# x loaded a second time, transposed, and scaled by GpSimd; half of k's maxima subtracted inside ScalarE's exp

## The reference

```python
xn = _ln(x, ln_w, ln_b)
q = xn @ Wq + bq
k = xn @ Wk + bk + (1.0 - src_mask) * -1000000.0
q = softmax(q.reshape(b, t, h, dh), axis=-1)      # 8 heads of 32 channels
k = softmax(k.reshape(b, t, h, dh), axis=1)       # over the 64 positions
v = ((xn @ Wv + bv) * src_mask).reshape(b, t, h, dh)
att = einsum('bnhd,bnhl->bhdl', k, v)
y = einsum('bnhd,bhdl->bnhl', q, att).reshape(b, t, d)
scale, shift = split((silu(emb) @ W_emb + b_emb)[:, None, :], 2, axis=2)
hh = _ln(y, ln2_w, ln2_b) * (1.0 + scale) + shift
out = x + silu(hh) @ W_out + b_out
```

## Time and profile before

| | |
|---|---|
| median of 3 runs | 322.28 us (321.87 to 325.95) |
| profiled execution, its time | 323.25 us |
| profiled execution, its span | 321.4 us |
| busy, TensorE / VectorE / GpSimd / ScalarE | 96% / 86% / 71% / 60% of the span |
| mean granted clock of TensorE | 0.992 of full speed |

### The profile page before, as it was taken

One profiled execution on the slowest core, in us unless ns is written; L12 is line 12 of the kernel. 1 busy time (PEld: TensorE's weight loads), 2 busy tenths in 40 slices (PEclk: granted clock), 3 DMA queues, 4 the chain that ended last, 5 costly groups with the idle time before them and its releaser, 6 DMA issues.

```text
span 321.4 us, 14568 instructions
## 1 busy us (share of the span) xinstructions
PE 308.0 (96%) x5664; PEld 263.4 (82%) x5664; DVE 275.1 (86%) x749; ACT 193.0 (60%) x378; POOL 229.4 (71%) x276
## 2 busy tenths in 40 slices
PE   7899989999999999999999999999999999999974
PEld 6577867887988898988888898988889898988864
DVE  3775989889797998989898989989898989988883
ACT  1449384667486575668485675757575765756360
POOL 2170459778778687878887787878788887889550
PEclk9999999999999999999999999999999999999979
DMA  7930301050412204040403214050403110010023
GB/s 213 353 110 0 100 4 37 2 167 4 130 38 72 92 8 155 2 163 0 131 32 97 66 42 121 0 163 0 145 19 119 44 65 0 12 55 2 4 68 131
DMA packets 21706, 23.84 MB, mean 74 GB/s; under 512 B 1073, under 2 KB 19121, under 8 KB 21682
## 3 DMA queue, kind: packets, MB, share of 16 engines
q1 hardware_dynamic: 20192, 21.89, 22.0%
q10 hardware_dynamic: 1490, 1.62, 1.5%
HBM read 15.12 MB, written 8.39 MB: 73 GB/s over the span
## 4 chain that ended last, share of the span: by engine, by line
PE 82%; DVE 7%; DMA 4%; issue 2%; ACT 1%; POOL 1%; SPq 1%; POOLq 1%; DVEq 0%
PE bv L890 27%; PE bk L890 27%; PE by L890 13%; PE by L966 4%; PE by L945 4%; PE bv L957 4%; PE by L1026 4%; DMA x_all<-in_x 4%; DVE ystat L769 1%; DVE xstat L621 1%; DVE y_s L760 1%; DVE xt_lo L789 1%; DVE k_t L800 1%; ACT xhat L550 1%; POOLq L45 1%
## 5 line engine op out<-in xcount | busy, mean ns | idle before, releaser
L349 POOL TENSOR_TENSOR k_t<-k_t,kmax 128x512 f32<-128x512 f32 x32 | 34.4, 1074 | 26.3 <-DVE kmax L804 26.3
L496 ACT ACTIVATE k_t<-k_t 128x512 f32<-128x512 f32 x32 | 20.0, 626 | 44.5 <-POOL k_t L349 44.5
L267 POOL TENSOR_TENSOR z_s<-z_s,mod_shift 128x512 f32<-128x512 f32 x30 | 30.7, 1043 | 14.2 <-DVE z_s L720 14.2
L360 POOL TENSOR_TENSOR h_lo<-h_s,h_hi 128x512 fp32r<-128x512 f32 x30 | 38.5, 1306 | 2.9 <-ACT h_hi L513 2.3
L368 POOL TENSOR_TENSOR x_all<-x_all,bo_all 128x1024 f32 (+1 forms) x16 | 38.9, 2434 | 0.0
L550 ACT ACTIVATE xhat<-x_all,xr 128x256 f32 (+1 forms) x62 | 32.2, 591 | 4.6 <-DVE xr L632 3.1
L416 POOL TENSOR_SCALAR y_s<-y_s,yr 128x256 f32<-128x256 f32 x60 | 32.7, 558 | 2.5 <-POOL yr L413 2.2
L800 DVE SCALAR_TENSOR_TENSOR k_t<-off,bk 128x512 f32<-128x512 f32 x32 | 21.9, 683 | 14.5 <-PE bk L890 14.5
L890 PE MATMUL bv<-w_o_hi,h_hi 128*128 128x256 f32 x120 | 32.3, 288 | 0.0
L890 PE MATMUL bv<-w_o_lo,h_hi 128*128 128x256 f32 x120 | 32.2, 290 | 0.0
L520 ACT ACTIVATE xt_hi<-by 128x512 fp32r<-128x512 f32 x32 | 17.4, 597 | 23.4 <-PE by L1026 23.4
(11 more groups left out here) (128 smaller groups left out, 867.2 us busy)
## 6 DMA issues: line engine op xcount, KB each, us to landing
x_all<-in_x SPq DMA_DIRECT2D x15, 512.0 KB, 4.6
out<-x_all SPq DMA_DIRECT2D x15, 512.0 KB, 3.2
off<-in_mask_rows SPq DMA_DIRECT2D x16, 256.0 KB, 3.3
x_all<-in_x SPq DMA_DIRECT2D x2, 256.0 KB, 3.7
z_s<-in_w_emb ACTq DMA_DIRECT2D x1, 512.0 KB, 9.7
h_s<-in_w_emb ACTq DMA_DIRECT2D x1, 512.0 KB, 12.3
out<-x_all SPq DMA_DIRECT2D x2, 256.0 KB, 2.6
y_s<-in_wk ACTq DMA_DIRECT2D x1, 256.0 KB, 3.8
```

Of the source, the lines that this page charges most:

```text
L267: return eng.tensor_tensor(z, z, mod_shift[:, c, span(g, GB)].unsqueeze(2).broadcast_to([P, GB, SEQ]), ALU.add)
L349: nc.gpsimd.tensor_tensor(kk, kk, kmax[:, c, :].unsqueeze(2).broadcast_to([P, GB, SEQ]), ALU.subtract).then_inc(ksub_d, 1)
L360: nc.gpsimd.tensor_tensor(h_lo[:, c, :], h_s[:, c, :], h_hi[:, c, :].bitcast(fp32), ALU.subtract).then_inc(hlo_d, 1)
L496: nc.scalar.activation(k_t[:, parity, c, :], k_t[:, parity, c, :], ACT.Exp).then_inc(kexp_d, 1)
```

## The change

x is handed over a second time, transposed in memory (x_t, channels by rows). Each group's block of it is loaded into xt_raw (channels in partitions). Rows now lie along the free dimension, so rstd and bias have to be the same in all partitions: xr[:,2:4], 128 partitions x 2 x 4 numbers, is stored to a small tensor in memory (rows_stored), and loaded again as a broadcast to all partitions (rows_loaded, 128 x 2 x 512). GpSimd multiplies and adds in place (x_scaled, two instructions for each block c), ScalarE copies to xt_hi (x_high), VectorE subtracts to xt_lo. xhat and its transposes on TensorE remain for group 0 alone. The statistics of x and x_rstd are made for group i+3 in turn i, where it was i+1; x is loaded three groups ahead (S says that group i+3 exists).

For block 1 of k, the mask is applied with the sign turned, so that the tile holds -k; VectorE takes the minimum, which is minus the maximum of k. ScalarE subtracts inside the exp: eight activations of 64 columns, one for each batch, with scale -1 and the minimum as bias. k_shifted on GpSimd remains for block 0.

The four instructions that normalise y_s go from GpSimd to ScalarE (y_hat_all, at the head of the next turn), but for the last turn. The orders change: on GpSimd two shifts, k_shifted, h_low 0, x_scaled 0, h_low 1, x_scaled 1, y_scale, x_rstd of i+3, x_biased; on VectorE x_stats stands between the two h_products, x_low after q's tiles 2 and 3; on ScalarE y_hat_all leads and x_high ends the turn. Two more turns at the end are written out.

```diff
+            def rows_stored(g, parity):
+                wait(sp, xr_d, 4 * g + 4)
+                wait(sp, rows_in, 16 * g - 32)
+                sp.dma_start(rows_dram[parity].rearrange("k (t p) -> p k t", p=P), xr[:, 2:4, :], allow_slow_non_contiguous=True
+                             ).then_inc(rows_out, 16)
+            def rows_loaded(g, parity):
+                wait(sp, rows_out, 16 * g)
+                wait(sp, xs_d, 2 * g - 2)
+                sp.dma_start(rows[:, :, :].rearrange("p k n -> p (k n)").unsqueeze(1),
+                             rows_dram[parity:parity + 1].rearrange("o k n -> o (k n)").unsqueeze(0)
+                             .broadcast_to([P, 1, 2 * GT])).then_inc(rows_in, 16)
...
+            def body(i, par, N, F, B, O, S):        # SP
+                if S:
+                    if not (isinstance(i, int) and i < 0):
+                        wait(sp, xstat_d, 4 * i + 5)
+                    load_x(i + 3, 1 - par)
                 if N and not (isinstance(i, int) and i < 1):
-                    wait(sp, xstat_d, 4 * i)
-                    load_x(i + 1, 1 - par)
                     wait(sp, kadd_d, 2 * i)
                     load_off(i + 1, 1 - par)
+                if not (isinstance(i, int) and i + 2 >= G):
+                    rows_stored(i + 2, par)
                 if O and not (isinstance(i, int) and i < 3):
                     store(i - 3)
+                if not (isinstance(i, int) and i + 2 >= G):
...
+                        load_xt(i + 2, par)
+                    rows_loaded(i + 2, par)
...
+            def x_scaled(g, parity, c):             # GpSimd
+                if c == 0:
+                    wait(pool, rows_in, 16 * g)
+                    wait(pool, xt_in[parity], 8 * (g + parity))
+                xc = xt_raw[:, parity, c, :]
+                nc.gpsimd.tensor_tensor(xc, xc, rows[:, 0, :], ALU.mult).then_inc(xm_d, 1)
+                wait(pool, xm_d, 2 * g + c - 1)
+                nc.gpsimd.tensor_tensor(xc, xc, rows[:, 1, :], ALU.add).then_inc(xs_d, 1)
...
+                if O:                               # GpSimd's body
+                    shifts(i - 2)
+                k_shifted(i, par)
+                for c in range(C):
+                    if O:
+                        h_low(i - 2, c)
+                    if N:
+                        x_scaled(i + 1, 1 - par, c)
+                if B:
+                    y_scale(i - 1)
...
+                if S:
+                    x_rstd(i + 3)
+                if not last_turn(i):
                     x_biased(i)
...
+            def k_exp_shifted(g, parity):           # ScalarE
+                wait(act, kmax_d, 2 * g + 2)
+                for n in range(GB):
+                    kk = k_t[:, parity, 1, n * SEQ:n * SEQ + SEQ]
+                    last = nc.scalar.activation(kk, kk, ACT.Exp, scale=-1.0, bias=kmax[:, 1, n:n + 1])
+                last.then_inc(kexp_d, 1)
...
+            def k_masked(i, par, c):                # VectorE
...
+                nc.vector.scalar_tensor_tensor(k_t[:, par, c, :], off[:, par, :], (-1000000.0, 1000000.0)[c], bk_[c][:, :],
+                                               ALU.mult, (ALU.add, ALU.subtract)[c]).then_inc(kadd_d, 1)
...
+            def x_low(i, c, full):                  # VectorE; full is xt_raw[:, 1 - par, c, :], for group 0 bt[c]
+                wait(dve, hi_d, 2 * i + c + 1)
+                nc.vector.tensor_tensor(xt_lo[:, c, :], full, xt_hi[:, c, :].bitcast(fp32),
+                                        ALU.subtract).then_inc(lo_d, 1)
...
+                if B:                               # VectorE's body
+                    kv_scaled(i - 1)
+                if O:
+                    h_product(i - 2, 0)
+                if S:
+                    x_stats(i + 3, 1 - par)
+                if O:
+                    h_product(i - 2, 1)
...
-                if F:                               # TensorE's body
+                if first(i):
+                    pe.wait_ge(xhat_d, 4)
                     for c in range(C):
-                        if c == 0:
-                            wait(pe, xhat_d, 4 * i + 4)
-                        wait(pe, ys_d, 2 * (i - 2) + 2)
                         for t in range(T):
```

More of the change, by code:

```diff
@@ L298, in _ @@
             load_x(1, 1)
+            load_xt(1, 1)
             sp.dma_start(w_o, w_out.rearrange("(c p) n -> p c n", p=P)).then_inc(wo_in, 16)
@@ L828, in body @@
                     y_stats(i - 1, (0, 1, 2, 3))
-                if F:
-                    q_tiles(i, par, (2, 3))
+                q_max(i, (2, 3))
+                q_shifted(i, par, (2, 3))
+                if N:
+                    for c in range(C):
+                        x_low(i + 1, c, xt_raw[:, 1 - par, c, :])
                 if O and not last_turn(i):
```

312 lines of the change are left out of this document (166 added, 146 removed).

## The result

The changed kernel takes 453.81 us (448.33 to 454.46, 4 runs) beside 323.0 us for the kernel before in the same runs: 1.40 times as long, with a 95% interval from 1.385 to 1.414. It is slower by 130.8 us, where +8.8 was forecast. The profiled execution has a span of 452.6 us.

The account below looks back on a forecast made before the run. TensorE bounded the kernel before, and GpSimd would bound it after: +7.2 (loop) + 2.5 (start) - 0.9 (end) = +8.8 us on the 321.4 span, 330.2, or 331.1 us measured; range 314 to 341.

Parts of the forecast that it names:

- the trip through memory: Storing and reloading rstd and bias: landing 3.2 to 7 us, covered in steady turns, +2.5 us at the start.
- The fourth rival: Rows come later than x_scaled wants them, so it waits for DMA every turn: above 341 us, chance 0.04.
- Their cost is nothing while those 7 us hold: Steady turns: rows_loaded and SP's transfers behind it cost nothing within 7 us of slack; beyond, every microsecond is lost.
- GpSimd is the bound: Loop turns: GpSimd needs 18.5 us against 17.9 before, +0.6 in each of twelve turns, +7.2 us.
- Its sum, 16.8: GpSimd's work in a turn without contention: 11.6 us that stays plus 5.24 for x_scaled's multiplies and adds.
- Four encounters, +1.7: Two h_products and two x_low on VectorE hold GpSimd up: 0.6, 0.6 and together 0.5 us a turn.
- the rival of the missed hand-off: kv_scaled late, k_shifted before h_product, GpSimd idle 0.8 us before h_low: turns 19.3, 340.7 us, chance 0.13.
- The h_products "nearly all" under the power: Kernel before, steady turn: VectorE's h_products, 217.57 to 218.85, lie nearly all under GpSimd's 1.02 us power.
- TensorE alone at 17.04: TensorE stays the bound, the VectorE instructions hidden or the multiplies cheaper: turns 17.04, 313.5 us, chance 0.2.
- VectorE "stays just below": Loop turn: VectorE busy 16.3 us plus 0.4 of gaps leaves about 1.8 of 18.5 for waits on GpSimd.
- y_hat_all's loop "level, no slack": y_scale through y_hat_all and attention to kv_scaled ends at 20.4 us; the h_product wants 18.5 + 1.85.
- Start and end: Start +2.5 us (bounds 1.6 and 5.4) for the uncovered rows; end -0.9, TensorE regaining 0.87 in turn 15.

Follow-up runs that it names:

- a2: The changed kernel with each group's store sent as one 4 KB piece from a row of ones, so rows are constant: 341.33 us.
- e1: The changed kernel with the scattered store waiting for y_product from turn 1 on, the output store and xt_raw load still behind it: 382.02 us.
- a4: The changed kernel, whole computation, with VectorE transposing rstd and bias in 32x32 blocks and four DMAs storing 8 pieces of 128 bytes each: 341.56 us.
- e2: The changed kernel with the scattered store at its old place, but the output store and xt_raw load behind it waiting for y_product: 414.16 us.
- a3: The kernel before the change, with the scattered store of 1024 numbers added in each turn and read by nobody: 373.61 us.
- c1: a4 without the two adds of x_scaled on GpSimd, so the bias is left out: 326.93 us.
- b4: a4 with GpSimd's order changed to x_scaled 0, h_low 0, h_low 1, x_scaled 1: 334.29 us.
- c2: b4 with both copies to e_k put ahead of q's exp in the tail: 334.02 us.
- b2: The changed kernel with each of the 1024 4-byte pieces written into its own 512 bytes of memory, rows from a constant: 349.8 us.
- c5: The changed kernel with each of the 1024 4-byte pieces written into its own 64 bytes of memory, rows from a constant: 350.7 us.

## Why the prediction was wrong

**The step that failed** is "the trip through memory", in both halves. The landing, which I took at 3.2 to 7 us because the trace had no piece of four bytes, is 9.5. The fourth rival has late rows in every turn. But the rows come in time: GpSimd waits for them once, 4.5 us in turn 0, not in each turn. What failed is the sentence "Their cost is nothing while those 7 us hold": I asked who waits for the store, and never what it does to those who don't. The store costs 112.5 of the 130.8 us (a2 against the change). In the turn shown, attention takes 7.46 us instead of 1.3 (+6.2), and the first tile of q and v products behind it, at the lower clock until about 241.6, takes 4.4 us where e1 has 3.0 (+1.4). The start loses 26.4 us instead of 2.5. Of these, a4 keeps 6.4 without the scattered store. The other 20 are the store's, 11.4 of them as the longer wait for the load of x behind it on SP's queue (14.50 against 3.13), which I had called "wanted half a turn or more later" with a steady turn in mind. The rival closest in time, "above 341 us" at 0.04, is right about the number alone. A bound from both sides would have needed a cost upwards for the store's effect on others; I gave it none, and 4% to everything of this kind.

What the engines lack while they stand stays open. I took it for instructions. For that speak that TensorE stands without a semaphore to wait for, where its instructions are short and not where they are long (e1), and that it goes on when the store should have landed (e2). But the trace speaks against it. It does show fetches: the page lists the DMA packets that bring instructions on queues of their own (q8 and q14, 22 and 11 packets in the run). From 140 to 370 us, inside the hardware loop, there is none of them, and TensorE stands there all the same, for 47.9 us:

```profile
q1 hardware_dynamic: 22906, 20.04, 61.0%
```

```profile
PE by L996 <- issue: 47.9, 40, 5.7
```

The first row is all that the profile lists of DMA queues in that stretch, the second is TensorE's waits there (us in total, times, longest). So either instructions reach the engines in the loop by a way that the trace doesn't hold, or it is something else that goes with each instruction and needs memory. The recording of the trace itself is one such thing that I can't rule out: every time on record comes with a span and a granted clock, so there is no run without it. Also open are why the cost grows with the number of pieces at nearly the same landing, and what ScalarE and VectorE waited for in a3.

**The rest**, read on a4, whose steady turn looks like this (length, PE, PEld, DVE, ACT, POOL, clock, DMA share, GB/s):

```profile
163.73:182.43 18.70, 17.43 (x342) 14.66 (x341) 17.63 (x47) 13.25 (x30) 16.75 (x17) 1.00 0.39 126
```

The turn is 18.70 us; forecast 18.5. Loop +8.8 us (7.2), start +6.4 (2.5), end +4.1 (-0.9): 340.7 for a forecast span of 330.2. GpSimd in that turn:

```profile
163.78 1.56 POOL L438 TENSOR_TENSOR yr<-yr,neg_half 128x4 f32<-128x4 f32 x1
...
171.98 1.05 POOL L397 TENSOR_TENSOR k_t<-k_t,kmax 128x512 f32<-128x512 f32 x1
174.32 1.27 POOL L408 TENSOR_TENSOR h_lo<-h_s,h_hi 128x512 fp32r<-128x512 f32 x1 [1.29 <-ACT h_hi L601]
175.55 1.74 POOL L417 TENSOR_TENSOR xt_raw<-xt_raw,rows 128x512 f32<-128x512 f32 x1
177.37 1.30 POOL L419 TENSOR_TENSOR xt_raw<-xt_raw,rows 128x512 f32<-128x512 f32 x1
```

and VectorE:

```profile
163.79 1.43 DVE L834 TENSOR_TENSOR xt_lo<-xt_raw,xt_hi 128x512 fp32r<-128x512 f32 x2
...
172.15 1.43 DVE L865 SCALAR_TENSOR_TENSOR h_s<-th,z_s 128x512 f32<-128x512 f32 x1
...
175.09 1.04 DVE L865 SCALAR_TENSOR_TENSOR h_s<-th,z_s 128x512 f32<-128x512 f32 x1
```

- *GpSimd is the bound*: right in a4, as c1 shows. It has no idle time but the 1.29 us and hand-offs under 0.2.
- *Its sum, 16.8*: 18.68 us from one power (163.78) to the next (182.46), less 1.29 idle, 0.55 by which the power is longer than its 1.01, and 0.45 by which xt_raw is: 16.4. xt_raw undisturbed is 1.29 to 1.30, as taken.
- *Four encounters, +1.7*: GpSimd lost 1.0 to two of them, one x_low (the power, 1.56) and the second h_product (xt_raw, 1.74). The first h_product did not go ahead of k_shifted: it comes at 172.15, 0.17 after it, and waits (1.43 for 0.69). Then h_hi, and GpSimd idle for 1.29 us. That is the rival of the missed hand-off, whose mechanism was right and which I gave 0.13; its price was 0.8. So 18.70 is 16.4 + 1.0 + 1.3: that it is near my 18.5 is luck, since 0.7 less for encounters and 0.4 less for the sum made up for 1.3 of idle time. The Trainium skill ("SBUF — State Buffer", section "Who interferes with whom") has it that whoever comes first blocks the other for its whole length; the rows of h_product and xt_raw agree. The power doesn't always. In the earlier trace rows an h_product begins at 217.57, 0.42 us into the power, and neither is longer for it; in a4 the power and an x_low begin together, and the power is longer by 0.55.
- *The h_products "nearly all" under the power*: misread. The power ends at 218.17 and the h_products at 218.85, so half of their 1.28 us lies behind it, and that half held up the small multiply at 218.25 (0.67 us instead of 0.20). They were less well hidden before than I said.
- *TensorE alone at 17.04* (first rival): never reached. b4, made against the missed hand-off, has the idle time gone and the turn at 18.18:

```profile
159.46:177.64 18.18, 17.61 (x342) 14.70 (x341) 17.82 (x47) 13.13 (x31) 17.34 (x17) 1.00 0.40 130
```

VectorE is busy for 17.82 of it, and waits once, 0.17 us. In c1 GpSimd has two adds less to do (14.44 busy), and the turn is still 17.49, with VectorE busy for 17.13, no wait of it over 0.17, and TensorE busy for 17.33:

```profile
157.31:174.80 17.49, 17.33 (x342) 14.68 (x341) 17.13 (x47) 13.13 (x31) 14.44 (x15) 1.00 0.43 131
```

- *VectorE "stays just below"*: right in a4 (17.63 of 18.70, with waits of 0.56 and 0.26 us for TensorE), wrong by a little in b4. What it waits for GpSimd counts as busy: its two h_products take 1.31 and 1.53 us there for 0.69 each. With 0.36 us of gaps left, b4's turn is VectorE's as far as busy time tells. The chain that ended last goes through TensorE for half of that turn, so the two share it, and no run takes them apart.
- *ScalarE*: eight exps 2.0 us instead of 1.8, covered, as forecast. *y_hat_all's loop "level, no slack"*: right; TensorE waits 0.26 us for it, and the h_product comes 0.17 too late:

```profile
167.79 1.09 PE L1081 MATMUL bv<-ident,y_s 128*128 128x128 f32 x8 [0.26 <-ACT y_s L560]
```

- *Start and end*: both too cheap. In a4, turn 1 takes 21.1 us instead of 15.4, and the store is not its reason there (2.2 us to landing). From 35.35 on VectorE works through the rest of that turn with no wait over 0.15 us; why it has more to do there I didn't test. At the end I gave TensorE its 0.87 back, and forgot that the last turn has the same encounters: VectorE's two h_products take 3.50 us there, for 2.00 in the earlier trace rows. That is 1.5 of the 5.0 us; the rest I have no run for, since c2, which tried one order there, changed nothing.

## What to carry to other kernels

A small DMA is priced by its pieces and where they lie, not by its bytes: before writing single numbers that lie next to each other in memory, turn them on chip (0.20 us here) and write pieces of 128 bytes. The signature is "issue" idle in an engine with its operands ready. DMA engines that are busy while they move a fifth of what they did can go with it (the change), or be idle (e2). Look for the smallest store issued some 4 us earlier. And when a trace lacks an operation, bound its effect on the bystanders too, not only its own length.

## What the runs showed of the hardware

- 1024 adjacent 4-byte writes to memory land after 9.5 us, 7.5 of them after the last packet; 128 of them after 8.65; one piece of the same 4 KB after 1.24. At 64 bytes apart 3.9, with a load in flight beside them. The same 1024 pieces to SBUF cost the kernel nothing (340.5 beside 341.3).
- During it, engines stand without a semaphore that the profile shows: 75.6 us of TensorE's time here. The Trainium skill ("SBUF — State Buffer", section "Who interferes with whom") says that DMA never contends with a compute engine. For the ports of SBUF nothing here speaks against it; for a store to memory, a2 against the change does, with 112.5 us.
- During such a stand TensorE's granted clock falls to its lower level (0.50 from 235 to 236), and the products behind it begin there (1.22 us for a pair of 512-column products; 0.72 in e1, where it did not stand).
- The Trainium skill ("DMA: Bandwidth & Descriptors", section "Specifications") says that pieces under 512 bytes are written by read-modify-write. By that alone b2, c5 and the change would be alike, and they are 349.8, 350.7 and 453.8: how close the pieces lie matters, and their size much less (a2 has 341.3).
